# Attention sum with a fifth slot, experts' tiles gathered by a table of row numbers, message sum added straight into x

## The chip, the cores and the metric

One core of a Trainium2 chip runs the whole program. The metric is the device time of one execution in microseconds (us), the median of several. A core has five engines that run their own instruction streams: TensorE (PE, matrix products, results in PSUM), VectorE (DVE), ScalarE (ACT), GpSimd (POOL) and SyncE (SP), and 16 DMA engines that all queues share. Engines wait for one another by semaphores.

## The reference, cut to what matters

Two rounds of a graph network with a mixer and a feed-forward or expert layer, on 3125 nodes (rows) of 256 numbers with 50000 edges, sorted by their destination. Three parts matter here:

```
# first round: message sum
x = x + (normalised, weighted sum over the edges of rows of xn @ W) + mixer(xn)
# second round: attention over the edges
score = clip(einsum('ehd,ehd->eh', q[edge_dst], k[edge_src]) / sqrt(32), -10, 10)
ex = exp(score - smax[edge_dst]);  alpha = ex / segment_sum(ex)[edge_dst]
wv = segment_sum(alpha[:, :, None] * v[edge_src], edge_dst)
# last layer: a shared expert for all rows, and the best 2 of 8 experts per row
shared = gelu(x @ W1s + b1s) @ W2s + b2s
topw, topi = top_k(softmax(x @ Wr), 2);  topw = topw / sum(topw)
routed = sum over the two of topw * (gelu(x @ W1p[e] + b1p[e]) @ W2p[e] + b2p[e])
out = x + shared + routed
```

## The kernel before, in words

The 3125 rows lie in SBUF as T = 25 tiles of R = 125 partitions (`m.x`, `m.y`, `m.z`); J = 5 tiles are a chunk. The edges are G = 80 groups of J x R = 625. The program is a row of stages (`phase`), each a block in which every engine has its own loop; a barrier of all engines stands between stages.

**Start** (`graph_layers`, from L2857). SP loads x (L2861), then fills the DRAM table `pairs` with zeros by four transfers of 2 MB (L2865) from an area that DVE cleared (L2870). The stage ends when SP has issued all; POOL then writes the constants (L135 on), and `edge_tables` loads the edge lists (L182, L183), which DVE takes up at L189. The landings of x and of the fills are waited for after `edge_tables`.

**Message sum** (`message_sum`, L680). For each group POOL issues five indirect DMAs (L745), each of 125 gathered rows of 1 KB, into one of SLOTS = 4 slots. DVE writes the 0/1 matrix that says which edge goes to which of a tile's rows (`hot`, L769), PE multiplies it with the gathered rows (L812), and DVE adds the product to `summed` = `m.y` (`Adder.add`, L552), two visits behind PE. A group visits one or two tiles of destinations. Ahead of the loop stand a clearing of `m.y` (L752), one of PSUM (L753), and an iota of 3125 numbers on POOL (L738), ahead of the first index copies (L757). After the loop DVE adds `summed` times 1/sqrt(degree) to x in 25 instructions (L792). ACT and PE turn weights of later stages between the loop's five parts (`Turner`, loads L584, stores L613).

**Attention sum** (`attention_sum`, L1633). The same pattern with 2 KB rows of k and v in f32 (`gkv`, four slots; L1685). In turn n DVE multiplies q with k for group n+1 (L1818; q is picked by one-hots of ACT, L1732 and L1738, on PE, L1771 to L1784), reduces (L1823), clips (L1824), ACT takes the exponent (L1745), DVE copies the index for group n+3 (`next_index`, L1836) once PE is done with group n-1, writes the one-hot of group n (L1862), adds what PE summed (L552), and weighs v of group n+1 (L1830). PE sums group n (L1806). POOL gathers a group when its index is there. Ahead of it, q (3.2 MB, L1701) is loaded to SBUF from DRAM.

**Routing** (`routing`, L2337) scores the rows against the 8 experts and gives each of the 6250 (row, expert) pairs a place in a list in which each expert's pairs fill whole tiles of TN = 256, NT = 32 tiles in all (`m.place`, L2484).

**Experts** (`shared_and_experts`, L2488). POOL writes each row to its two places in the DRAM table `pairs` (L2534, 50 indirect DMAs). Meanwhile PE does SHARED_BEFORE = 3 chunks of the shared expert (`chunk`: up products L457 with gelu on ACT, L2696, and splitting into two f16 halves on DVE, L2749 and L2751; then down products, L2621, and DVE's addition to x, L2762). Then come the 32 tiles: SP loads rows (`load_rows`, L2562) and an expert's weights of 2 MB (L2552, four slots) ahead, PE turns the rows (`turn`, L2634; ACT copies them, L2703), and multiplies up and down; results go to DRAM (L2567). After the last tile PE does the other two chunks, POOL gathers the results of the two experts of every row back (L2544, GOT = 4 slots), and DVE joins them into x (`join`, L2771): seven tiles after the fourth chunk, the rest after the last. SP stores each tile of x when joined (L2599).

## Time and profile before

| | |
|---|---|
| median of 3 runs | 4137.75 us (4130.2 to 4140.1) |
| profiled execution | 4135.46 us, span 4133.7 us |
| busy: PE, DVE, ACT, POOL | 2615.2, 2172.5, 1260.5, 1312.0 us |
| start and edge tables | 0 to 130 |
| message sum | 253 to 914 |
| attention sum | 2388 to 3251 |
| routing | 3515 to 3558 |
| experts | 3558 to the end |

The profile is of one execution. Times in its rows are microseconds from the span's start unless a mean in ns is meant. The stage bounds above are read from the order of time. Where a row names a releaser (`<-`), that is what ended the idle time of the engine ahead of the instruction. Idle time of an engine that isn't what ends last costs nothing.

### The profile page before, as it was taken

Reading aid. Unit: us, or ns where it says so; the run is one execution under the profiler, and the core shown is the slowest. Engines: PE = TensorE matmul, PEld = TensorE weight load, DVE = VectorE, ACT = ScalarE, POOL = GpSimd, SP = SyncE. Lnnn points to the kernel's source line nnn. Section 1 sums busy time; section 2 is a strip of 40 time slices with the busy share of each in tenths; the row PEclk is TensorE's granted clock in tenths of the full one; section 3 lists DMA queues with packets and bytes.
Section 4 is the critical chain, followed back from the end, with each engine's and each line's share of the span. In section 5 each row is a group of like instructions: output and inputs, shape, how many; then the busy total and the mean of one; then the engine's idle time right before and its main releaser. Section 6 shows DMA issues by size and latency. Waiting matters only on the chain. (4 is left out here: it accounts for less than half of the span.)

```text
span 4133.7 us, 66642 instructions
## 1 busy us (share of the span) xinstructions
PE 2615.2 (63%) x17072; PEld 2109.2 (51%) x17073; DVE 2172.5 (53%) x4422; ACT 1260.5 (30%) x2441; POOL 1312.0 (32%) x996
## 2 busy tenths in 40 slices
PE   3513334437587799975654426666766487699993
PEld 2413333324276577753444325445545466589983
DVE  5623323231555488883347736666666655544443
ACT  0200000003244155551477512222222244244440
POOL 0038888842000000000001136667767500510015
PEclk9955555557688699987777658999888778799996
DMA  2036566730000000002000046666665100356643
GB/s 116 23 93 161 144 170 159 193 86 6 0 21 0 15 15 15 15 8 100 14 1 0 0 120 159 159 163 168 168 165 161 54 21 0 126 177 231 232 162 85
DMA packets 263746, 383.33 MB, mean 93 GB/s; under 512 B 122411, under 2 KB 189607, under 8 KB 258810
## 3 DMA queue, kind: packets, MB, share of 16 engines
q0 software_dynamic: 156960, 171.31, 16.8%
q1 hardware_dynamic: 93850, 199.08, 14.5%
q10 hardware_dynamic: 12864, 12.06, 1.0%
q8 instruction: 36, 0.59, 0.1%
q14 instruction: 36, 0.29, 0.0%
HBM read 318.81 MB, written 62.55 MB: 92 GB/s over the span
## 5 line engine op out<-in xcount | busy, mean ns | idle before, releaser
L1685 POOL DMA_INDIRECT as_gkv<-gather_kv,as_index x415 | 565.7, 1363 | 280.5 <-DVE as_index L1836 170.5
L745 POOL DMA_INDIRECT ms_got<-gather,ms_index x400 | 505.9, 1265 | 128.6 <-issue 109.3
L812 PE MATMUL ms_total<-ms_got,ms_hot 125*125 125x256 f16 x1040 | 231.7, 411 | 382.8 <-DMA ms_got<-gather,ms_index 292.9
L812 PEld LDWEIGHTS ms_total<-ms_got,ms_hot 125*125 x1040 | 203.6, 219 | 411.1 <-issue 411.1
L1806 PE MATMUL as_total<-as_gkv,as_hot 125*125 125x264 f32 x1040 | 280.0, 420 | 76.1 <-DVE as_summed L552 66.1
L2093 POOL MEMSET bm_fx<- 128x128 f32 x1 | 0.2, 204 | 1012.9 <-POOLq L114 1012.9
L1806 PEld LDWEIGHTS as_total<-as_gkv,as_hot 125*125 125x125 f32 x1040 | 201.2, 202 | 127.6 <-issue 91.4
L1479 ACT ACTIVATE ex_h<-ex_up,ex_now 128x313 f32<-128x313 f32 (+1 forms) x320 | 195.8, 612 | 197.6 <-PE ex_up L457 190.4
L2749 DVE CAST moe_hidden<-moe_h 128x256 f16<-128x256 f32 (+1 forms) x336 | 107.3, 319 | 206.2 <-ACT moe_h L2696 206.2
L1818 DVE TENSOR_TENSOR z_flat<-as_picked,as_gkv 125x1280 f32<-125x1280 f32 x81 | 120.4, 1487 | 176.7 <-DMA as_gkv<-gather_kv,as_index 130.2
L2696 ACT ACTIVATE moe_h<-moe_up,moe_w 128x256 f32<-128x256 f32 (+1 forms) x336 | 163.2, 486 | 140.3 <-PE moe_up L457 95.4
L1771 PE MATMUL as_picked<-y_rows,as_zeros 125*125 125x512 f16 (+1 forms) x246 | 72.5, 412 | 205.0 <-DVE z_flat L1818 147.3
L2544 POOL DMA_INDIRECT z_rows<-results,place x50 | 64.8, 1295 | 418.1 <-DMA results<-moe_made 374.3
L1780 PE MATMUL as_picked<-y_rows,as_pick 125*125 x1060 | 168.5, 316 | 44.5 <-issue 40.0
L1780 PEld LDWEIGHTS as_picked<-y_rows,as_pick 125*125 x1060 | 140.0, 155 | 80.2 <-issue 77.8
L2659 PE MATMUL moe_down<-moe_w,moe_hidden 128*128 128x256 f16 x1536 | 178.2, 273 | 0.0
L1745 ACT ACTIVATE as_gkv<-as_score 125x40 f32<-125x40 f32 x81 | 19.1, 236 | 510.8 <-DVE as_score L1824 510.8
L457 PE MATMUL moe_up<-moe_cols,moe_w 128*128 128x256 f16 x1536 | 172.9, 273 | 1.4 <-ACT moe_cols L2703 1.4
L1521 DVE TENSOR_TENSOR ex_h<-ex_h 128x313 f16<-128x313 f32 (+1 forms) x320 | 155.3, 485 | 11.0
L457 PEld LDWEIGHTS moe_up<-moe_cols,moe_w 128*128 128x128 f16 x1536 | 150.0, 98 | 19.1 <-issue 1.6
L670 ACT ACTIVATE ms_split<-ms_raw 128x1024 f16<-128x1024 f32 x36 | 37.6, 1054 | 399.7 <-DMA ms_raw<-in_L_ffn_W1p 358.8
L2659 PEld LDWEIGHTS moe_down<-moe_w,moe_hidden 128*128 128x128 f16 x1536 | 150.5, 98 | 17.2
(431 smaller groups left out, 5859.1 us busy)
## 6 DMA issues: line engine op xcount, KB each, us to landing
moe_w<-wsplit SPq DMA_DIRECT2D x34, 2052.0 KB
as_dsts<-in_dst SPq DMA_DIRECT2D x83, 305.2 KB
wsplit<-ms_split SPq DMA_DIRECT2D x36, 512.0 KB, 4.3
pairs<-z_flat SPq DMA_DIRECT2D x4, 2048.0 KB, 21.5
ms_raw<-in_L_ffn_W1p SPq DMA_DIRECT2D x16, 512.0 KB, 6.9
ms_raw<-in_L_ffn_W2p SPq DMA_DIRECT2D x16, 512.0 KB, 9.2
moe_rows<-pairs SPq DMA_DIRECT2D x32, 256.0 KB
results<-moe_made SPq DMA_DIRECT2D x32, 256.0 KB, 8.2
```

Of the source, the lines that this page charges most:

```text
L457: ins = pe.matmul(out, left(k, b), right(n, b), start=(i == 0), stop=(i == len(todo) - 1))
L745: pool.indirect_dma_start(out=got[:, s, j, :], out_offset=None, in_=m.gather0, in_offset=bass.IndirectOffsetOnAxis(ap=index[:, s, j:j + 1] ...
L812: ins = pe.matmul(total[:, visit % RING, 0:C], hot[:, visit % RING, j, :], got[:, s, j, p * C:(p + 1) * C], start=(j + p == 0), stop=(j + ...
L1479: act.activation(h32[:, u % 4, 0:n], up[:, u % 4, 0:n], ACT.Relu, bias=now[:, 1, layer, o:o + 1], scale=now[:, 0, layer, o:o + 1]).then_in ...
L1521: dve.tensor_tensor(to[:, 1, o, at:at + n], full, to[:, 0, o, at:at + n], ALU.subtract).then_inc(s_h, 1)
L1685: pool.indirect_dma_start(out=gkv[:, s, j, 0:2 * C], out_offset=None, in_=m.gather_kv, in_offset=bass.IndirectOffsetOnAxis(ap=index[:, s, ...
L1780: ins = pe.matmul(picked[:, j // 2, at:at + C], pick[:, visit % PICKS, j * R:(j + 1) * R], q16[:, tile, p, :], start=False, stop=False)
L1806: ins = pe.matmul(total[:, visit % RING, 0:W], hot[:, s, j, :], gkv[:, s, j, C:C + W], start=(j == 0), stop=(j == J - 1))
L1818: dve.tensor_tensor(qk[:, :].rearrange("p (j c) -> p j c", j=J), picked[:, :, :].rearrange("p b c -> p (b c)")[:, 0:J * C] .rearrange("p ( ...
L2659: ins = pe.matmul(down[:, h, 0:C], hidden[:, k, f, h * 128:(h + 1) * 128], part(s, r, 1, f, 0, C), start=False, stop=(f == FB - 1 and n == 2))
L2696: act.activation(h32[:, u % 4, 0:n], up[:, u % 4, 0:n], ACT.Gelu, scale=1.0 / WS, bias=bias(s, f)).then_inc(s_h32, 1)
L2749: dve.tensor_copy(hidden[:, 0, f, at:at + n], full).then_inc(s_hhigh, 1)
```

## The change

1. The fills of `pairs`, the table itself and the clearing behind them go. `x` is the only load of the first stage.
2. Message sum: `Adder` takes a scale and adds straight into `m.x`; `m.y` isn't cleared, the pass L792 goes, and the one-hot is made from `m.row_no` plus a tile's first number, so that the long iota becomes one of 25.
3. Attention sum: five slots. Four lie in `gkv`, the fifth in an unused part of `z_cols`. ACT's loop has ten turns in its body, since its other buffers alternate by two.
4. Routing stores the rows (`m.rows16`) to the DRAM table `gather0` and splits each place into a block of 128 and a place in it (`m.spot`).
5. Experts: after the first shared chunk DVE and ACT make one-hots from `m.spot`, PE multiplies them (50 matmuls) into a table that holds the row number for each of the 8192 places, and POOL gathers each tile's rows by it, two indirect DMAs per tile, four slots. SHARED_BEFORE is 2, so that three chunks come after the experts. GOT is 12, and the joins stand between the units of the last three chunks.

```diff
-SHARED_BEFORE = 3
+SHARED_BEFORE = 2
+BLOCKS = NT * HN
...
-        dve.tensor_tensor(into, into, fresh, ALU.add).then_inc(self.s_added, 1)
+        if self.scale is None:
+            dve.tensor_tensor(into, into, fresh, ALU.add).then_inc(self.s_added, 1)
+        else:
+            dve.scalar_tensor_tensor(out=into, in0=fresh, scalar=self.scale[:, bass.ds(oldest, 1)], in1=into,
+                                     op0=ALU.mult, op1=ALU.add).then_inc(self.s_added, 1)
...
-        node_no = ph.sb("node_no", [R, N])
+        node = ph.sb("node", [R, T])
...
-                pool.iota(node_no[:, :], pattern=[[1, N]], base=0, channel_multiplier=0,
+                pool.iota(node[:, :], pattern=[[R, T]], base=0, channel_multiplier=0,
...
-                dve.memset(summed[:, :, :], 0.0).then_inc(s_zero, 1)
...
-                            dve.tensor_tensor(hot[:, visit % RING, :, :],
-                                              repeat_mid(node_no[:, bass.ds(tile * R, R)], J),
-                                              repeat_last(m.edge_dst[:, g, :], R), ALU.is_equal)\
-                                .then_inc(s_hot, 1)
+                            dve.scalar_tensor_tensor(out=hot[:, visit % RING, :, :],
+                                                     in0=repeat_mid(m.row_no[0:R, :], J),
+                                                     scalar=node[:, bass.ds(tile, 1)],
+                                                     in1=repeat_last(m.edge_dst[:, g, :], R),
+                                                     op0=ALU.add, op1=ALU.is_equal).then_inc(s_hot, 1)
...
-                with dve.Fori(0, CHUNKS) as c:
-                    for j in range(J):
-                        t = c * J + j
-                        dve.scalar_tensor_tensor(out=m.x[:, t, :], in0=summed[:, t, :],
-                                                 scalar=m.inv_sqrt_degree[:, bass.ds(t, 1)], in1=m.x[:, t, :],
-                                                 op0=ALU.mult, op1=ALU.add).then_inc(s_zero, 1)
...
+        SLOTS = 5
+        index = ph.sb("index", [R, SLOTS, J], I32)
         W = C + X8
-        index = ph.sb("index", [R, SLOTS, J], I32)
-        gkv = ph.sb("gkv", [R, SLOTS, J, C + W])
+        most = ph.sb("gkv", [R, SLOTS - 1, J, C + W])
+
+        at = J * R // 2 + 1
+        gkv = [most[:, s, :, :] for s in range(SLOTS - 1)]
+        gkv.append(m.z_cols[0:R, 1, at:at + J * (C + W)].rearrange("p (j w) -> p j w", j=J))
...
-                with act.Fori(0, G // SLOTS) as i:
-                    for s in range(SLOTS):
-                        n = i * SLOTS + s
+                with act.Fori(0, G // (2 * SLOTS)) as i:
+                    for s in range(2 * SLOTS):
+                        n = i * (2 * SLOTS) + s
                         bounds = group_bounds(act, m, n + 3)
                         weights(n + 1, (s + 1) % SLOTS)
-                        one_hots(n + 3, i * 2 + (s + 3) // 2, (s + 3) % 2, bounds)
+                        one_hots(n + 3, i * SLOTS + (s + 3) // 2, (s + 3) % 2, bounds)
 
             @block.tensor
...
+                sp.dma_start(m.gather0.rearrange("(t p) n -> p t n", p=R),
+                             m.rows16.rearrange("p t k c -> p t (k c)")).then_inc(s_rows, 16)
...
+                v.link(dve.tensor_scalar(m.spot[:, 0, :, :], stat[:, :, :], 1.0 / 128, 0.5 / 128 - 0.5,
+                                         ALU.mult, ALU.add))
+                v.link(dve.tensor_scalar(m.spot[:, 0, :, :], m.spot[:, 0, :, :], RNE, RNE, ALU.add, ALU.subtract))
+                v.link(dve.scalar_tensor_tensor(out=m.spot[:, 1, :, :], in0=m.spot[:, 0, :, :], scalar=-128.0,
+                                                in1=stat[:, :, :], op0=ALU.mult, op1=ALU.add))
...
-        GOT = 4
+        GOT = 12
...
-                for t in range(T):
-                    for k in range(2):
+                pool.iota(number[:, :], pattern=[[1, 128]], base=0, channel_multiplier=0,
+                          allow_small_or_imprecise_dtypes=True).then_inc(s_number, 1)
+                pool.iota(own[:, :], pattern=[[0, 1]], base=0, channel_multiplier=1,
+                          allow_small_or_imprecise_dtypes=True).then_inc(s_number, 1)
+                pool.wait_ge(s_taken, 1)
+                for i in range(NT):
+                    s = i % RINGW
+                    if i >= RINGW:
+                        pool.wait_ge(s_turned, i - RINGW + 1 + AHEAD)
+                    for h in range(HN):
+                        at = i * HN + h
                         pool.indirect_dma_start(
-                            out=m.pairs, out_offset=bass.IndirectOffsetOnAxis(ap=m.place[:, k, t:t + 1], axis=0),
-                            in_=rows16[:, t, :, :].rearrange("p k c -> p (k c)"), in_offset=None).then_inc(s_spread, 16)
-                pool.wait_ge(s_spread, 32 * T)
...
-                def load_rows(i, s):
-                    sp.dma_start(rows[:, s, :, :], m.pairs.rearrange("(i h p) n -> p i h n", h=HN, p=128)
-                                 [:, bass.ds(i, 1), :, :].rearrange("p i h n -> p (i h) n")).then_inc(s_rows[s], 16)
...
+                    if c == 0:
+                        pe.wait_ge(s_marked, T + 1)
+                        pe.wait_ge(s_block, 1 + J)
+                        pe.wait_ge(s_added, J + AHEAD)
+                        for n in range(2 * T):
+                            k, t = n // T, n % T
+                            ins = pe.matmul(down[:, 2, 0:2 * BLOCKS], in_block[:, k, t, :],
+                                            marked[:, k, t, :, :].rearrange("p a n -> p (a n)"),
+                                            start=(n == 0), stop=(n == 2 * T - 1))
+                        ins.then_inc(s_inverse, 1)
+                        pe.wait_ge(s_taken, 1)
...
+                    if c == 0:
+                        act.wait_ge(s_number, 2)
+                        act.wait_ge(s_block, 1)
+                        act.activation(marked[:, :, :, 0, :].rearrange("p k t n -> p (k t) n"),
+                                       of_block[:, :, :, :].rearrange("p k t n -> p (k t) n"), ACT.Copy,
+                                       scale=own[:, 0:1]).then_inc(s_marked, 1)
+                        for t in range(T):
+                            act.activation(marked[:, :, t, 1, :], of_block[:, :, t, :], ACT.Copy,
+                                           scale=float(t)).then_inc(s_marked, 1)
...
+                def blocks(j):
+
+                    some = slice(j * 2 * T // J, (j + 1) * 2 * T // J)
+                    if j == 0:
+                        dve.wait_ge(s_number, 2)
+                        dve.tensor_tensor(of_block[:, :, :, :].rearrange("p k t n -> p (k t) n"),
+                                          repeat_mid(number[0:R, 0:BLOCKS], 2 * T), repeat_last(spots[0], BLOCKS),
+                                          ALU.is_equal).then_inc(s_block, 1)
+                    dve.tensor_tensor(in_block[:, :, :, :].rearrange("p k t n -> p (k t) n")[:, some, :],
+                                      repeat_mid(number[0:R, :], 2 * T // J), repeat_last(spots[1][:, some], 128),
+                                      ALU.is_equal).then_inc(s_block, 1)
...
-                    add(c)
+                    add(c, blocks if c == 0 else None)
+                    if c == 0:
+                        dve.wait_ge(s_inverse, 1)
+                        dve.tensor_copy(row_of[:, :], down[:, 2, 0:BLOCKS]).then_inc(s_set, 1)
+                        dve.wait_ge(s_set, 2)
+                        dve.scalar_tensor_tensor(out=row_of[:, :], in0=down[:, 2, BLOCKS:2 * BLOCKS], scalar=float(R),
+                                                 in1=row_of[:, :], op0=ALU.mult, op1=ALU.add).then_inc(s_set, 1)
+                        dve.wait_ge(s_set, 3)
+                        dve.tensor_copy(taken[:, :], row_of[:, :]).then_inc(s_taken, 1)
...
+                joins = iter(range(T))
+
+                def join_next(u):
+
+                    if u % 2 == 1:
+                        t = next(joins)
+                        join(t, 0)
+                        join(t, 1)
+
                 for c in range(SHARED_BEFORE, CHUNKS):
                     dve.wait_ge(s_down, c * J + AHEAD)
-                    halves_of(UB + NT * FB + (c - SHARED_BEFORE) * units, units, of_chunk)
+                    dve.wait_ge(s_added, c * J + AHEAD)
+                    halves_of(UB + NT * FB + (c - SHARED_BEFORE) * units, units, of_chunk,
+                              join_next if c > SHARED_BEFORE else lambda u: u >= units // 2 and join_next(u))
                     add(c)
-                    upto = T if c == CHUNKS - 1 else T * (c + 1 - SHARED_BEFORE) // (AFTER + 1)
-                    if c == CHUNKS - 1:
-                        dve.wait_ge(s_added, CHUNKS * J + AHEAD)
-                    for t in range(done, upto):
-                        join(t, 0)
-                        if t > done:
-                            join(t - 1, 1)
-                    join(upto - 1, 1)
-                    done = upto
+                dve.wait_ge(s_added, CHUNKS * J + AHEAD)
+                for t in joins:
+                    join(t, 0)
...
-        FILLS = 4
-        with nc.semaphore("x_in") as s_x, nc.semaphore("clear") as s_clear, nc.semaphore("filled") as s_filled:
+        with nc.semaphore("x_in") as s_x:
             with nc.Block() as block:
 
                 @block.sync
                 def _(sp):
                     sp.dma_start(m.x[:, :, :], a["x"].rearrange("(t p) n -> p t n", p=R)).then_inc(s_x, 16)
-                    sp.wait_ge(s_clear, 1)
-                    for i in range(FILLS):
-                        n = NT * TN // FILLS
-                        sp.dma_start(m.pairs[i * n:(i + 1) * n, :].rearrange("(p k) n -> p (k n)", p=128),
-                                     z_flat[:, 0:n * 2 * C // 256].bitcast(F16)).then_inc(s_filled, 16)
-
-                @block.vector
-                def _(dve):
-                    dve.memset(z_flat[:, 0:NT * TN // FILLS * C // 128], 0.0).then_inc(s_clear, 1)
```

## Rows read from the trace of the kernel before

**Rows 1.** Order of time, 0 to 60: start, duration, engine, line, operation [idle before].

```profile
0.81 0.36 SPq L2861 DMA_DIRECT2D x_rows<-in_x  x1
...
5.23 23.12 SPq L2865 DMA_DIRECT2D pairs<-z_flat  x4
28.76 0.20 POOL L135 MEMSET ident<- 128x128 f32 x1 [27.50 <-POOLq L2857]
...
50.92 0.81 DVE L189 CAST edg_rawf<-edg_raw 80x1250 f32<-80x1250 int32 x1 [45.71 <-DMA edg_raw<-in_src]
```

**Rows 2.** Busy by engine in stretches: us, PE, PEld, DVE, ACT, POOL, clock, DMA share, GB/s.

```profile
10.00:20.00 10.00, 0.00 (x0) 0.00 (x0) 0.00 (x0) 0.00 (x0) 0.00 (x0) 1.00 0.34 118
...
2450.00:3236.00 786.00, 519.45 (x2560) 397.06 (x2560) 505.12 (x610) 189.75 (x289) 547.45 (x400) 0.89 0.61 162
...
4040.00:4080.00 40.00, 26.56 (x195) 20.97 (x193) 21.16 (x52) 8.35 (x16) 20.64 (x16) 0.79 0.29 78
```

**Rows 3.** Order of time, 250 to 264, ahead of the message sum's loop.

```profile
253.99 5.39 DVE L752 MEMSET y_rows<- 125x6400 f32 x1 [17.55 <-issue]
...
262.88 1.38 POOL L745 DMA_INDIRECT ms_got<-gather,ms_index  x1 [7.08 <-DVE ms_index L757]
```

**Rows 4.** Groups by line, 264 to 900: count | busy us, mean ns | idle before.

```profile
L745 POOL DMA_INDIRECT ms_got<-gather,ms_index x400 | 505.9, 1265 | 128.6 <-issue 109.3 <-DVE ms_index L779 12.2 <-DVE ms_index L757 7.1
...
L769 DVE TENSOR_TENSOR ms_hot<-ms_node_no,edge_dst x104 | 84.5, 812 | 103.0 <-issue 103.0
```

**Rows 5.** Order of time, 890 to 915, end of the message sum.

```profile
894.26 2.36 PE L812 MATMUL ms_total<-ms_got,ms_hot 125*125 125x256 f16 x10 [5.40 <-DMA ms_got<-gather,ms_index]
...
897.89 9.98 DVE L792 SCALAR_TENSOR_TENSOR x_rows<-y_rows,inv_sqrt_degree,x_rows  x25 [0.47 <-DVE y_rows L552]
...
909.57 0.37 ACTq L613 DMA_DIRECT2D turned_res<-ms_cols  x1
```

**Rows 6.** Groups by line, 2450 to 3236, the loop of the attention sum.

```profile
L1685 POOL DMA_INDIRECT as_gkv<-gather_kv,as_index x400 | 547.5, 1369 | 275.7 <-DVE as_index L1836 170.5 <-issue 105.3
...
L1818 DVE TENSOR_TENSOR z_flat<-as_picked,as_gkv 125x1280 f32<-125x1280 f32 x80 | 118.9, 1487 | 130.7 <-DMA as_gkv<-gather_kv,as_index 130.2 <-PE as_picked L1784 0.4
...
L1862 DVE SCALAR_TENSOR_TENSOR as_hot<-row_no,as_node,edge_dst 125x625 f32<-125x625 f32 x104 | 90.7, 872 | 124.5 <-PE as_total L1806 80.4 <-issue 44.0
```

**Rows 7.** Order of time, 2806 to 2809, inside that loop.

```profile
2806.10 1.48 DVE L1830 TENSOR_TENSOR as_gkv<-as_gkv 125x1280 f32<-125x1280 f32 x1
...
2806.31 2.35 POOL L1685 DMA_INDIRECT as_gkv<-gather_kv,as_index  x1 [0.30 <-issue]
```

**Rows 8.** Order of time, 2388 to 2455 and 3240, the loop's edges.

```profile
2388.72 0.29 SPq L1701 DMA_DIRECT2D y_rows<-gather_q  x1
...
2436.43 1.32 PE L1771 MATMUL as_picked<-y_rows,as_zeros 125*125 125x512 f16 x3 [57.56 <-DMA y_rows<-gather_q]
...
2454.12 1.65 POOL L1685 DMA_INDIRECT as_gkv<-gather_kv,as_index  x1 [41.67 <-DVE as_index L1836]
...
3240.04 0.36 DVE L1874 TENSOR_SCALAR as_gkv<-as_summed 125x200 f32<-125x200 f32 x1 [7.66 <-DMA as_gkv<-gather_kv,as_index]
```

**Rows 9.** Chain that ended last, 3550 to 4134: start, us, what.

```profile
3636.79 11.02 PE moe_down L2621 x99
```

**Rows 10.** Groups by line, 3480 to 4134.

```profile
L2703 ACT ACTIVATE moe_cols<-moe_turned 128x1024 f16<-128x1024 f16 x32 | 32.7, 1023 | 15.2 <-PE moe_turned L2634 13.4
...
L2771 DVE SCALAR_TENSOR_TENSOR x_rows<-z_rows,share,x_rows 125x256 f32<-125x256 f32 x50 | 21.5, 482 | 42.4 <-DMA z_rows<-results,place 42.4
```

**Rows 11.** Order of time, 4013 to 4017, after the last expert tile.

```profile
4013.56 12.97 PE L457 MATMUL moe_up<-z_flat,moe_w 128*128 128x313 f16 x96 [0.52 <-issue]
...
4016.56 1.38 POOL L2544 DMA_INDIRECT z_rows<-results,place  x1 [374.28 <-DMA results<-moe_made]
```

**Rows 12.** Order of time, 4082 to 4134, the end.

```profile
4082.69 0.42 DVE L2762 SCALAR_TENSOR_TENSOR x_rows<-moe_down,x_rows 125x256 f32<-125x256 f32 x1 [2.20 <-PE moe_down L2621]
...
4127.94 1.28 DVE L2771 SCALAR_TENSOR_TENSOR x_rows<-z_rows,share,x_rows 125x256 f32<-125x256 f32 x3 [1.38 <-DMA z_rows<-results,place]
```

74 lines of the change are left out of this document (42 added, 32 removed).

## The prediction

> **What bounds the kernel now.** I read the page first (slices and chain), then one stage at a time: the list of costly lines and waits inside each stage the change touches, and the order of time at the stage's edges. The program is a row of stages with a barrier between them, so what counts is what ends last in each.
>
> Start: the load of x is issued at 0.81, four fills of `pairs` hold SP's queue from 5.23 to 28.35, POOL starts its constants only at 28.76, and VectorE (DVE) gets the edge lists at 50.92 after 45.71 us of waiting for that load [rows 1]. While x is alone, the DMA engines are busy 0.34 of the time and move 118 GB/s [rows 2].
>
> Message sum: POOL's 400 gathers take 505.9 us, with 109.3 us between them and 19.3 us of waits on DVE [rows 4], in a loop of 634 us. POOL is the bound; work of DVE there is hidden. At the stage's end the DVE pass over x (897.89 to 907.87) ends before the weight turner's last store is even issued, at 909.57, and the turner hangs on TensorE's (PE's) last group at 894.26 [rows 5].
>
> Attention sum: 786 us for 80 groups (2450 to 3236 [rows 2]), 9.8 per group. POOL is busy 547.5, between gathers 105.3, and waits 170.5 for an index [rows 6], 41.7 of it at the start [rows 8]; DVE waits 130.2 for gathered rows [rows 6]. Each waits for the other: a ring too short, no engine full. An index for group n+3 is written in the middle of turn n, and its rows are wanted at the start of turn n+2. With a period P that leaves 2P less some 3.5 us; the gather takes 5 x 1.63 on POOL, about 1 to start and 4.3 to land after the last (below), some 14 to 15.5 with queueing: P of 9 to 9.5, near the 9.8 seen.
>
> Experts: PE is full from the first chunk to the experts' end at 4013.04; then two chunks of shared work with joins, the last addition at 4083.11, and 18 tiles still to join; the last join ends at 4129.2, the span at 4133.7 [rows 9, 11, 12]. The tail is POOL's gathers and the wait of DVE for them.
>
> **Part by part.**
>
> *Fills of `pairs` gone.* The first stage's barrier now waits for nothing long, so the edge lists are asked for near 4 to 5 us instead of 31. What is late next is x's load: 3.2 MB at 118 GB/s [rows 2] is 27.1 us, from about 3 us on; the edge lists lie behind it in the same queue and land at about 32. Gain 50.9 - 32 = 19. Ends: 14 if the load begins slowly, 38 if the lists get past x (then only barriers and a short load remain, some 13 us). I take 19. The share of 0.34 is 5.4 of 16 engines [rows 2]; the Trainium skill, "DMA: Bandwidth & Descriptors", section "Why a DMA increments its semaphore by 16 and not by 1", says that a transfer is spread over the largest k up to 16 that divides both slowest dims, so 125 partitions get 5, and 80 get 16. By that rule the lists' packets on those 5 engines queue behind x; the row agrees with 5 engines.
>
> *Message sum, front.* The memset of y (5.39) goes from in front of the index copies [rows 3]; the 3125-wide iota, which ran beside it, goes too. All gathers start 5.4 earlier, and POOL-bound work keeps that. In the loop the one-hot becomes a scalar_tensor_tensor (872 ns each in the attention sum [rows 6] against 812 now [rows 4]), 104 x 0.06 = 6 us on an engine with slack: 0. The addition with a scale costs some 0.06 more, hidden by the same POOL work; with the cover gone it would be 6 + 6 us. The DVE pass of 9.98 at the end is worth 0, because the turner ends later [rows 5]. Sum -5.4, ends -8 and +10 (the second if the new one-hot lengthens POOL's gathers by 0.15 each time).
>
> *Attention sum, fifth slot.* Now 3P less 3.5 must cover the same 15.5: 6.3, no bound any more. DVE alone would need 786 - 130 = 656 us, 8.2 per group. POOL: a gather that nothing disturbs is 1.21 (the shortest; the mean in the message sum is 1.265 [rows 4]) plus 0.30 between [rows 7], 1.51; it is longer when a DVE instruction with two SBUF inputs runs as it starts: 2.35 at 2806.31, begun 0.21 after L1830 [rows 7]. The mean is 1.369 [rows 6], the excess over 1.21 400 x 0.159 = 63.6 us, met while POOL was active for (547.5 + 105.3) / 786 = 0.83 of the loop; active all the time it meets 63.6 / 0.83 = 76. So POOL needs 400 x 1.51 + 76 = 680, more than DVE's 656: POOL becomes the bound, at 8.5 per group. It starts that loop at 2454.12 [rows 8], later by what a fourth group of gathers costs the load of q: that load would take 27 us alone (3.2 MB at 118 GB/s [rows 2]) and took 47.7 beside 15 gathers (2388.72 to 2436.43 [rows 8]), 1.4 us for each, so 5 more cost 6.9. POOL ends at 2454.1 + 6.9 + 680 = 3141.0. The rows land 4.3 later: from the first gather of the loop at 2454.12 to the end of the last wait at 3240.04 [rows 8] are 785.9 us, of which 547.5 + 105.3 is POOL's work and 128.8 its waits in the loop (170.5 - 41.7). So 3145.3 against 3240.0, -94.7. I give back 3 for turns with two visits, in which DVE is late: -92 (rounded). The fourth unused group at the end is in the 400. Ends: -125 (DVE the bound at 656, with its tail) and -55 (P stays at 9.1).
>
> The Trainium skill's "SBUF — State Buffer", section "Who interferes with whom", says that a DVE instruction with two SBUF inputs contends with a GpSimd instruction that reads SBUF. The trace agrees (2.35 against 1.21). By it the gain is 12 us smaller than with POOL's present mean.
>
> *Routing.* Three DVE operations on 50 columns, each waited for, at the end: one on 200 columns takes 0.36 (L1874 [rows 8]), so at most 1.1 for three, and +0.7 taken for 50 columns each, ends 0.3 and 1.5. The store of 3.2 MB of rows takes some 28 us at the pace of rows 2, and the stage is 43 us long by the table ahead: 0; uncovered, up to 5.
>
> *Experts, one shared chunk moved behind.* A chunk is 12.97 up [rows 11] and 120 x 11.02/99 = 13.3 down [rows 9]: -26.3 ahead of the experts.
>
> *Experts, table of row numbers.* From the end H of the first chunk's DVE halves: `of_block` has 3200 columns at 1.16 ns (1485 for 1280 [rows 7]; 872 for 625): 3.6. Then ACT: one of 3200 at 0.8 to 1.0 ns, 2.8, and 25 of 128 at 0.31 (between a fixed 0.2 and 1023 for 1024 [rows 10]): 7.8. Ready at H + 14.2, while PE's down phase ends at H + 11.1 [rows 9]. 50 matmuls at 0.11 at most [rows 9]: 5.5. Three small DVE operations with waits 1.2. PE goes on at H + 20.9, +9.8; ends 6 and 16 (slower small ACT instructions, lower clock). The gathers of rows, 2 for each tile, run four tiles ahead on an idle POOL with 11.4 us per tile ((4013.0 - 3647.8) / 32 [rows 9, 11]): 0.
>
> *Tail, from T = 4013.04.* DVE's unit is 0.85 beside gathers, a tile's two joins 0.96 [rows 10]. POOL starts at T+3.5 [rows 11] and gives a tile each 3.4 us. Third-to-last chunk: the first join waits for T+11.2, the fourth ends T+22.4, halves end 23.3, PE's down 34.5. The next two: 1.5 + 16 x 0.85 + 8 x 0.96 + 11.0 = 33.8 each, to T+102.1. Then 0.5, five tiles 4.8, the last store 4.5 (as now): T+112 against T+120.7, -9. Ends -16 and +20. The twelve slots let POOL finish near T+90, so it no longer ends last.
>
> **Sum.** -19 - 5.4 - 92 + 0.7 - 26.3 + 9.8 - 9 = -141.2. The profiled run took 4135.46 for a span of 4133.7; 4135.5 - 141.2 = 3994.3, and the median shown, 4137.75, is 2.3 above that run: **3996**.
>
> **Rivals.**
> *Port costs nothing more (P down to DVE's 8.2).* For it: the two engines may fall in step, as they do now where DVE works while POOL waits. -125 in the attention sum instead of -92: 3963. Against: 185 DVE instructions with two SBUF inputs have nowhere to hide.
> *Edge lists pass x.* -38 instead of -19: 3977.
> *PE's clock falls in the tail.* Joins leave PE idle in each up phase, 8 to 10 us. Down phases at half speed: 3 x 11 = 33, and up phases that end 4 later: +45, 4041. For it: between 4040 and 4080, where PE stands still for some 13 us, the granted clock is 0.79 on the mean, so part of it at the lower of the two levels, 1.2 instead of 2.4 GHz [rows 2]. Against: the new stalls come in pieces under 2 us.
> *Fifth slot brings nothing* (landings lengthen with the load, or a hidden wait of PE or ACT takes over): 3996 + 92 = 4088. For: PE is 519 us busy of 786, DVE 505. Against: neither is near the whole, and the DMA share is 0.61 [rows 2].
> *Slower than before: the experts' weights come late.* Rows in 1 KB pieces on POOL's queue share the 16 DMA engines with 2 MB of weights for every tile. It decides when a tile's weights need more than 11.4 us; at 15.9 per tile, 32 x 4.5 = 144 us, the whole gain is gone: 4140, and any more is slower. Against: now the same rows and weights are read, and PE takes 365 us for the 32 tiles, from 3647.81 [rows 9] to 4013.04 [rows 11], with hardly a gap.
>
> **How the numbers follow.** Forecast 0.60 (3970 to 4022), port rival 0.09, edge lists 0.08, clock in the tail 0.14, nothing from the slot 0.06, weights 0.03 (half of it slower). The range 3962 to 4036 leaves out the last two, and part of the clock's. What a measurement here can tell from no change is 0.3%, 12 us: faster 0.97, same 0.01, slower 0.02.
>
> **What would show it.** DVE's first edge operation at 32; message sum's first gather 24 us earlier, near 238.5, its last DVE pass gone and the end still the turner's; POOL in the attention sum waiting under 10 us for indices in the loop, a mean above 1.40 us, DVE's wait for rows down to some 40, loop near 690; a hole of 8 to 11 us on PE after the first chunk; PE's end 4 to 8 us before the span's. It is wrong if POOL still waits for indices, or if the tail after the experts takes over 121.

## The result, and the profile after

The changed kernel takes **3985.89 us** (median of 4 runs, 3984.23 to 3990.22), the kernel before 4138.93 in the same comparison (4130.20 to 4141.86): ratio 0.9635, 95% interval 0.9618 to 0.9652. The forecast was 3996 with a range of 3962 to 4036. The profiled execution took 3987.43 for a span of 3985.7, 148.0 less than before.

How much earlier the changed kernel is at the edges of the stages:

| edge | before | after | earlier by | of it in this stretch |
|---|---|---|---|---|
| DVE's first edge operation [rows 1] | 50.92 | 31.94 | 19.0 | -19.0 |
| message sum, first gather [rows 3] | 262.88 | 237.58 | 25.3 | -6.3 |
| message sum, turner's last store [rows 5] | 909.57 | 885.45 | 24.1 | +1.2 |
| attention sum, first gather | 2389.98 | 2370.07 | 19.9 | +4.2 |
| attention sum, end of the last wait [rows 8] | 3240.04 | 3121.01 | 119.0 | -99.1 |
| routing, start | 3514.92 | 3395.17 | 119.7 | -0.7 |
| experts, first turned tile | 3647.65 | 3507.11 | 140.5 | -20.8 |
| experts, end (T) | 4013.04 | 3872.50 | 140.5 | 0.0 |
| span's end | 4133.7 | 3985.7 | 148.0 | -7.5 |

Order of time, changed kernel, 0 to 34 and 234 to 239 (start, duration, engine, line, operation [idle before]); these answer to [rows 1, 3]:

```profile
0.81 0.35 SPq L2931 DMA_DIRECT2D x_rows<-in_x  x1
...
1.62 0.20 POOL L136 MEMSET ident<- 128x128 f32 x1 [0.36 <-POOLq L2927]
...
4.23 20.72 SPq L183 DMA_DIRECT2D edg_raw<-in_dst  x1
25.00 0.42 SPq L184 DMA_DIRECT2D edg_raw<-in_src  x1
31.94 0.81 DVE L190 CAST edg_rawf<-edg_raw 80x1250 f32<-80x1250 int32 x1 [31.82 <-DMA edg_raw<-in_src]
...
234.50 1.76 DVE L757 MEMSET ms_total<- 125x2048 f32 x1 [16.52 <-PEq L115]
...
236.30 0.31 DVE L761 COPY ms_index<-edge_src 125x5 int32<-125x5 int32 x3
237.58 1.38 POOL L750 DMA_INDIRECT ms_got<-gather,ms_index  x1 [2.94 <-DVE ms_index L761]
```

The first stage no longer waits for the fills (POOL's constants stand at 1.62 instead of 28.76), and DVE gets the lists at 31.94, as forecast. One thing wasn't in the forecast: behind x's load the issue of the first list alone holds SP's queue for 20.72 us, so the second list is only asked for at 25.00.

The attention sum, groups by line, 2430 to 3125 (count | busy us, mean ns | idle before and what ended it). The fifth slot lies in `z_cols`, which the view names `z_flat`, so its gathers and products have lines of their own; together they answer to [rows 6]:

```profile
L1689 POOL DMA_INDIRECT as_gkv<-gather_kv,as_index x320 | 437.7, 1368 | 102.3 <-issue 94.6 <-DVE as_index L1840 7.8
L1689 POOL DMA_INDIRECT z_flat<-gather_kv,as_index x80 | 110.2, 1377 | 63.9 <-DVE as_index L1840 39.7 <-issue 24.2
...
L1822 DVE TENSOR_TENSOR z_flat<-as_picked,as_gkv 125x1280 f32<-125x1280 f32 x65 | 96.6, 1485 | 72.6 <-PE as_picked L1788 52.0 <-DMA as_gkv<-gather_kv,as_index 20.1 <-issue 0.5
...
L1866 DVE SCALAR_TENSOR_TENSOR as_hot<-row_no,as_node,edge_dst 125x625 f32<-125x625 f32 x104 | 90.6, 871 | 120.5 <-issue 61.7 <-PE as_total L1810 58.8
...
L1822 DVE TENSOR_TENSOR z_flat<-as_picked,z_flat 125x1280 f32<-125x1280 f32 x16 | 23.8, 1485 | 3.4 <-DMA z_flat<-gather_kv,as_index 3.4
```

POOL's waits for an index fell from 128.8 us in the loop to 7.8 (the 39.7 are the start), DVE's for rows from 130.2 to 23.5 (20.1 + 3.4). POOL is at work nearly all the time: 437.7 + 110.2 busy and 94.6 + 24.2 between gathers. The edges, order of time [rows 8]:

```profile
2368.82 0.29 SPq L1705 DMA_DIRECT2D y_rows<-gather_q  x1
...
2422.08 1.32 PE L1775 MATMUL as_picked<-y_rows,as_zeros 125*125 125x512 f16 x3 [63.12 <-DMA y_rows<-gather_q]
...
2439.86 1.65 POOL L1689 DMA_INDIRECT z_flat<-gather_kv,as_index  x1 [39.68 <-DVE as_index L1840]
...
3113.10 1.21 POOL L1689 DMA_INDIRECT as_gkv<-gather_kv,as_index  x1 [0.31 <-issue]
3121.01 0.36 DVE L1878 TENSOR_SCALAR as_gkv<-as_summed 125x200 f32<-125x200 f32 x1 [13.27 <-DMA as_gkv<-gather_kv,as_index]
```

From PE's first matmul to the start of POOL's last gather, "the loop" below, it is 798.0 us before and 691.0 after. In the traces of the fills back, the lists first, q in two transfers, both of these together and the chunk in front (all below), whose loops have the same instructions, it is 683.5 to 696.3: a difference of under some 13 us between two loops shows nothing by itself.

The table of row numbers and the tail, order of time, changed kernel [rows 9, 11, 12]:

```profile
3469.64 5.08 ACT L2758 ACTIVATE z_rows<-rowvec 125x128 f16<-125x128 f16 x25
...
3475.55 2.95 PE L2694 MATMUL moe_down<-z_rows 125*128 125x128 f16 x50 [0.61 <-DVE x_rows L2820]
...
3479.31 2.97 PE L458 MATMUL moe_up<-z_flat,moe_w 128*128 128x313 f16 x21 [0.81 <-DVE moe_taken L2845]
...
3869.83 2.67 PE L2680 MATMUL moe_down<-moe_w,moe_hidden 128*128 128x256 f16 x23
...
3875.99 1.45 POOL L2577 DMA_INDIRECT z_rows<-results,place  x1 [63.00 <-DMA results<-moe_made]
...
3907.02 0.42 DVE L2820 SCALAR_TENSOR_TENSOR x_rows<-moe_down,x_rows 125x256 f32<-125x256 f32 x1 [2.20 <-PE moe_down L2642]
...
3941.68 0.42 DVE L2820 SCALAR_TENSOR_TENSOR x_rows<-moe_down,x_rows 125x256 f32<-125x256 f32 x1 [2.20 <-PE moe_down L2642]
...
3975.54 0.42 DVE L2820 SCALAR_TENSOR_TENSOR x_rows<-moe_down,x_rows 125x256 f32<-125x256 f32 x1 [2.19 <-PE moe_down L2642]
3976.00 4.67 DVE L2829 SCALAR_TENSOR_TENSOR x_rows<-z_rows,share,x_rows 125x256 f32<-125x256 f32 x10
```

PE stands for 0.61 + 0.81 and works 2.95 for the table, a hole of 4.4. T, the end of the experts' last matmul, is 3872.50 here. The last additions of the three chunks end at T+34.9, T+69.6 and T+103.5, then five tiles are joined without a wait.

### The profile page after: what moved, and what is told of

It is laid out like the page before. It is cut to its first block and busy times, and to the rows that moved or that the text cites. A ratio compares the mean times of both kernels' runs of the same rounds, so it can differ in the third digit from the quotient of the medians.

```text
span 3985.7 us, 66521 instructions
## 1 busy us (share of the span) xinstructions
PE 2587.3 (65%) x17122; PEld 2086.2 (52%) x17123; DVE 2170.5 (54%) x4408; ACT 1269.1 (32%) x2467; POOL 1315.5 (33%) x1017
## 3 DMA queue, kind: packets, MB, share of 16 engines
q1 hardware_dynamic: 87700, 185.50, 14.2%
## 5 line engine op out<-in xcount | busy, mean ns | idle before, releaser
L750 POOL DMA_INDIRECT ms_got<-gather,ms_index x400 | 506.2, 1265 | 124.9 <-issue 114.4
L1689 POOL DMA_INDIRECT as_gkv<-gather_kv,as_index x340 | 462.0, 1359 | 108.7 <-issue 100.9
L1810 PE MATMUL as_total<-as_gkv,as_hot 125*125 125x264 f32 x850 | 218.8, 406 | 78.0 <-DVE as_summed L555 65.6
L1810 PEld LDWEIGHTS as_total<-as_gkv,as_hot 125*125 125x125 f32 x850 | 157.7, 193 | 117.8 <-issue 91.8
L1784 PE MATMUL as_picked<-y_rows,as_pick 125*125 x1060 | 150.3, 291 | 52.6 <-issue 47.7
L1784 PEld LDWEIGHTS as_picked<-y_rows,as_pick 125*125 x1060 | 123.9, 141 | 87.3 <-issue 84.5
L2567 POOL DMA_INDIRECT moe_rows<-gather,moe_taken x64 | 63.0, 984 | 309.9 <-PE moe_turned L2655 259.8
L1866 DVE SCALAR_TENSOR_TENSOR as_hot<-row_no,as_node,edge_dst 125x625 f32<-125x625 f32 x104 | 90.6, 871 | 120.5 <-issue 61.7
L2793 DVE TENSOR_TENSOR moe_hidden<-moe_h,moe_hidden 128x256 f16<-128x256 f32 (+1 forms) x336 | 148.3, 441 | 11.6
L458 PE MATMUL ex_down<-ex_w,ex_h 128*125 128x256 f16 x1200 | 148.1, 276 | 2.3
```

The costliest lines, as they stand in the source:

```text
L458: ins = pe.matmul(out, left(k, b), right(n, b), start=(i == 0), stop=(i == len(todo) - 1))
L750: pool.indirect_dma_start(out=got[:, s, j, :], out_offset=None, in_=m.gather0, in_offset=bass.IndirectOffsetOnAxis(ap=index[:, s, j:j + 1] ...
L1689: pool.indirect_dma_start(out=gkv[s][:, j, 0:2 * C], out_offset=None, in_=m.gather_kv, in_offset=bass.IndirectOffsetOnAxis(ap=index[:, s, ...
L1784: ins = pe.matmul(picked[:, j // 2, at:at + C], pick[:, visit % PICKS, j * R:(j + 1) * R], q16[:, tile, p, :], start=False, stop=False)
L1810: ins = pe.matmul(total[:, visit % RING, 0:W], hot[:, s, j, :], gkv[s][:, j, C:C + W], start=(j == 0), stop=(j == J - 1))
L2793: dve.tensor_tensor(hidden[:, 1, f, at:at + n], full, hidden[:, 0, f, at:at + n], ALU.subtract).then_inc(s_hidden, 1)
```

## The experiments

Every ratio is to the kernel before, run on the same chip in the same comparison; the changed kernel's is 0.9635. Trace numbers are of one profiled execution each.

**One part back: four slots**

```
-        SLOTS = 5
+        SLOTS = 4
```

> The changed kernel with four slots in the attention sum in place of five (the fourth then lies in z_cols). Theory: the ring's length was the bound. POOL waits for indices again, near 130 us in the loop, DVE for rows near 130 us; the loop takes 785 us in place of 687, the whole 4085 us (4078 to 4092). Rival: the stage got faster through the place of the slots or through its start; then the loop stays under 720 and the whole under 4015.

Measured: 4107.02, ratio 0.9908 (0.9882 to 0.9934), the loop 806.1.

```profile
L1689 POOL DMA_INDIRECT as_gkv<-gather_kv,as_index x253 | 350.2, 1384 | 163.2 <-DVE as_index L1840 95.7 <-issue 67.5
...
L1822 DVE TENSOR_TENSOR z_flat<-as_picked,as_gkv 125x1280 f32<-125x1280 f32 x52 | 77.4, 1488 | 69.2 <-DMA as_gkv<-gather_kv,as_index 67.6 <-issue 0.7 <-PE as_picked L1788 0.4
```

(Groups by line, 2430 to 3110; the gathers and products of the fourth slot are lines of their own.) Both old waits are back: over the whole loop POOL waits 129.3 us for indices, near the 130 expected. The slot alone carries 0.027 of the ratio, some 113 of the 153 us, and the rival that it brings nothing falls, as does the one that the place of the slots or the start did it. The loop is 21 us and the total 22 us longer than expected, outside the range given; why, no run shows.

**Is DVE the next bound?** The reduction over 1280 numbers is left out, 40 of its inputs are copied instead.

```
-   v.link(dve.tensor_reduce(score[:, :], qk[...], AX_X, ALU.add))
+   v.link(dve.tensor_copy(score[:, :], qk[:, 0:J * X8]))
```

> The changed kernel, with the reduction of q*k in the attention sum left out (the scores are 40 columns of the product, copied; 1.3 us less of DVE in each of 80 turns). Theory: POOL is the bound now, so the loop stays at 677 to 692 us, DVE's waits for rows grow by about 100 us, the whole is 3976 to 3992. Rival: DVE is the bound; then the loop falls by about 100 us to 585, the whole to 3885.

Measured: 3993.61, ratio 0.9635 (0.9609 to 0.9662); the loop 697.4. DVE has 102 us less to do (some 80 times 1486 to 224 ns), and nothing is gained; loop and total end just above the expected 692 and 3992. The number fits POOL as the bound, and DVE's work isn't it. But POOL waits 28.5 us for indices in the loop here, and DVE has new waits (below), so the run alone doesn't prove it.

**The port's price taken away.** The weights of `weigh` are ones in PSUM, so that this instruction has one SBUF input.

```
-   dve.tensor_tensor(rows, rows, repeat_last(gkv[s][:, :, 2 * C:C + W], HD), ALU.mult)
+   dve.tensor_tensor(rows, rows, repeat_mid(spare[:, 0:C], J), ALU.mult)
```

> The changed kernel, where the weighing of v multiplies by ones in PSUM instead of by the exponents in SBUF (same size, one SBUF input instead of two; v is not weighed). Theory: DVE instructions with two SBUF inputs lengthen the gathers that start beside them. POOL's mean falls from 1.37 to 1.22 to 1.27 us, POOL needs about 620 us, DVE and PE bound the loop at 645 to 665, the whole is 3950 to 3967. Rival: the gathers are long because the DMA queue is full; then the mean stays near 1.37, the loop near 687, the whole near 3986.

Measured: 4020.25, ratio 0.9699 (0.9671 to 0.9727): a miss. The first half, the shorter gathers, holds. These are the groups of the loop, 2430 to 3110:

```profile
L1690 POOL DMA_INDIRECT as_gkv<-gather_kv,as_index x301 | 377.5, 1254 | 151.3 <-issue 88.6 <-DVE as_index L1840 62.7
...
L1867 DVE SCALAR_TENSOR_TENSOR as_hot<-row_no,as_node,edge_dst 125x625 f32<-125x625 f32 x100 | 88.0, 880 | 137.0 <-remote 60.1 <-PE as_total L1811 41.1 <-issue 35.8
```

The mean gather fell from 1368 to 1254 ns, about 46 us over 400. It came back as POOL's waits for an index (83.6 us in the loop instead of 7.8), and the loop took 718.4, 27.4 more. The Trainium skill, "SBUF — State Buffer", section "Who interferes with whom", says that a DVE instruction with two SBUF inputs contends with a GpSimd instruction that reads SBUF, as a gather reads its index there; the mean here agrees, but what the stage gains isn't in that rule.

**The fills back.** Four transfers of 2 MB and their clearing, as in the kernel before, to a table that nothing reads.

```
+   for i in range(FILLS):
+       sp.dma_start(m.pairs[i * n:(i + 1) * n, :]..., z_flat[...].bitcast(F16)).then_inc(s_filled, 16)
```

> The changed kernel with the four fills of 2 MB back in the first stage (and the clearing ahead of them; nothing reads them). Theory: the fills alone held the edge lists; DVE's first edge operation is at 50.9 again, the whole is 19 us longer, 4005 (4001 to 4009). Rival: the load of x bounds the start in both; then the whole stays at 3986 to 3990.

Measured: 4004.48, ratio 0.9658 (0.9634 to 0.9682). DVE's first edge operation is at 50.95 and the first gather of the message sum at 256.58, both 19.0 later than in the changed kernel. The span is 8.7 longer only, since the same loop of the attention sum took 683.5 in this execution instead of 691.0. So the 19 us are shown by the trace; the ratios (0.0023 apart, intervals that overlap) don't tell 9 from 19.

**q in two transfers**

```
-   sp.dma_start(q16..., m.gather_q...).then_inc(s_q, 16)
+   for lo, hi in ((0, 120), (120, R)):
+       sp.dma_start(q16...[lo:hi], m.gather_q...[lo:hi]).then_inc(s_q, 16)
```

> The changed kernel with the load of q in the attention sum cut in two transfers, partitions 0 to 119 and 120 to 124 (3.2 MB in all, as before). Theory (a transfer of 125 partitions runs on few of the 16 DMA engines, 0.34 of their time and 118 GB/s in the rows of before, while 80 or 120 partitions spread over more): q lands 10 to 30 us after the stage's first gather instead of 53, the loop's first gather comes 25 to 40 us sooner, the ratio to the kernel before falls from 0.9635 to 0.954 to 0.958. Rival (q is late because the gathers of four groups take the DMA engines' time, whichever way q is cut): q still lands after 48 to 55 us and the ratio stays at 0.9635.

Measured: 3976.46, ratio 0.9596 (0.9564 to 0.9628): between the two. Busy in the stretch 2380 to 2390 (us, PE, PEld, DVE, ACT, POOL, clock, DMA share, GB/s), first the changed kernel, then this one:

```profile
2380.00:2390.00 10.00, 0.00 (x0) 0.00 (x0) 0.00 (x0) 0.00 (x0) 7.86 (x8) 0.50 0.83 208
```

```profile
2380.00:2390.00 10.00, 0.00 (x0) 0.00 (x0) 0.00 (x0) 0.00 (x0) 7.86 (x8) 0.50 1.12 195
```

The share adds up the times of packets, which overlap, so it can pass 1. In these 10 us SP's queue, that of the load, moved 0.81 MB instead of 0.39, and POOL's gathers 1.14 instead of 1.70: the load got more, but out of the gathers' part, and the sum didn't rise. q is there 35 us after the first gather instead of 52. Then PE waits for something else, 8.86 us:

```profile
2405.03 1.32 PE L1776 MATMUL as_picked<-y_rows,as_zeros 125*125 125x512 f16 x3 [46.17 <-DMA y_rows<-gather_q]
...
2412.79 0.82 ACT L1737 ACTIVATE z_flat<-as_dsts,as_minus_node 125x625 bf16<-125x625 int32 x1 [47.80 <-DMA as_dsts<-in_dst]
...
2415.21 2.36 PE L1785 MATMUL as_picked<-y_rows,as_pick 125*125 x10 [8.86 <-ACT as_pick L1743]
```

The destination numbers, asked for behind q, land last; the loop's first gather comes 12 us sooner, not 25 to 40.

**Edge lists ahead of x**

```
+   sp.dma_start(raw[:, 0, :], a["dst"]...).then_inc(s_lists, 16)
+   sp.dma_start(raw[:, 1, :], a["src"]...).then_inc(s_lists, 16)
    sp.dma_start(m.x[:, :, :], a["x"]...).then_inc(s_x, 16)
```

> The changed kernel with the two edge lists (0.8 MB) asked for ahead of x in the first block. Theory (the lists were late only because they stood behind x in the same queue): DVE's first edge operation at 7 to 12 us instead of 31.9, everything after it 20 to 25 us sooner, ratio 0.9575 to 0.959. Rival (x is what the next stage needs as well, so it only moves the wait to the layernorm): first edge operation early, but the message sum's first gather still at 237 and the ratio at 0.9635.

Measured: 3964.06, ratio 0.9578 (0.9543 to 0.9613), as expected. Order of time of this kernel, 0 to 6:

```profile
0.81 0.40 SPq L2926 DMA_DIRECT2D raw_lists<-in_dst  x1
1.26 0.41 SPq L2927 DMA_DIRECT2D raw_lists<-in_src  x1
1.73 0.35 SPq L2928 DMA_DIRECT2D x_rows<-in_x  x1
...
5.17 0.81 DVE L184 CAST edg_rawf<-raw_lists 80x1250 f32<-80x1250 int32 x1 [5.06 <-PEq L115]
```

The first gather of the message sum is at 211.26, 26.3 sooner: nothing of it is lost. The lists land before the barriers are through.

**The shared chunk back in front**

```
-SHARED_BEFORE = 2
+SHARED_BEFORE = 3
```

> The changed kernel with three shared chunks ahead of the experts and two behind, as the kernel before had it; the rest of the change stays. Theory: ahead of the experts +26.3; behind them the tail loses one chunk of 33.8 us, but POOL, which gathers a tile's two rows in 3.4 us, then sets the end at T+3.5+85 and 13 tiles are left to join, so T+97 instead of T+113, -16; total +10, ratio 0.9660. Rival (the tail follows PE alone, the joins are not the limit): T+80, total -7, ratio 0.962. Rival 2 (my +26.3 is wrong since something else, say the experts' weights, set the experts' start): ratio 0.9595.

Measured: 3994.51, ratio 0.9642 (0.9611 to 0.9674). The experts end at 3899.2, 26.7 later (expected +26.3), the span at T+94.9 (expected T+97). DVE's last joins wait for POOL again:

```profile
3987.36 1.00 DVE L2829 SCALAR_TENSOR_TENSOR x_rows<-z_rows,share,x_rows 125x256 f32<-125x256 f32 x2 [2.23 <-DMA z_rows<-results,place]
3988.70 1.01 DVE L2829 SCALAR_TENSOR_TENSOR x_rows<-z_rows,share,x_rows 125x256 f32<-125x256 f32 x2 [0.33 <-DMA z_rows<-results,place]
```

So taking the move back costs 26.7 - 18.3 = 8.4 us in the span, less than the comparison of the ratios can show: most of the gain ahead of the experts is paid again behind them.

**Both edits together**

> Both edits together, edge lists ahead of x and the load of q cut in 120 + 5 partitions. If both theories hold the gains add: 45 to 65 us under the changed kernel, ratio 0.948 to 0.9525. If only the lists' holds: 0.958.

Measured: 3948.14, ratio 0.9537 (0.9505 to 0.9569), just above the expected 0.948 to 0.9525. The span is 39.4 us shorter than the changed kernel's; the lists' run alone gave 25.1 and q's 8.9, together 34 of the 39.4.

**A busier PE**, once with ones in PSUM, once in the changed kernel. Eight matmuls of zeros in each turn, into a bank that is overwritten:

```
    pick_q(n + 2, ahead)
+   next_visit = pe.snap(before)
+   pe.wait_ge(s_added, next_visit + 1)
+   for _ in range(8):
+       pe.matmul(total[:, next_visit % RING, 0:C], zeros[:, :], q16[:, 0, 0, :], start=True, stop=True)
```

> The kernel with weigh's second input in PSUM again (ones instead of the weights), plus eight matmuls of 256 columns with zero weights in each turn of the attention sum, between the picked rows and the sum of the turn, into a bank of `total` that is free by then and is overwritten afterwards; only TensorE gets more work. Theory (the gathers' shorter mean did not pay there because TensorE, standing still more often, ran 19 of 99 visits at the lower clock and DVE waits for each): slow visits fall to under 8, the loop ends 25 to 45 us sooner than without the eight, ratio 0.959 to 0.964 against 0.9699. Rival (the waits of 5 to 6.7 us come from elsewhere, say the POOL's index arriving late, and the slow matmuls only follow from them): slow visits fewer, but the loop as long or longer, ratio 0.9695 or more.

> The changed kernel with the same eight matmuls a turn and nothing else. Theory (POOL is the bound and only 6 of 100 visits are slow, 9 us in all): between 9 us faster and 3 us slower, ratio 0.961 to 0.9645. Rival (TensorE's own time is on the path in each turn): 80 x 0.9 = 70 us slower, ratio 0.980.

Measured: 3974.01, ratio 0.9600 (0.9569 to 0.9631), and 3982.45, ratio 0.9629 (0.9600 to 0.9658). With ones in PSUM the loop falls from 718.4 to 681.4. Busy in 2450 to 3050, ones in PSUM without and with the eight:

```profile
2450.00:3050.00 600.00, 427.24 (x2200) 327.21 (x2201) 438.91 (x521) 161.75 (x246) 429.90 (x343) 0.93 0.74 182
```

```profile
2450.00:3050.00 600.00, 485.72 (x2906) 384.70 (x2905) 458.72 (x548) 171.70 (x261) 453.08 (x362) 0.98 0.79 192
```

In the changed kernel the granted clock is 0.97 over the same stretch, 0.99 with the eight, and PE's busy time rises there from 428.6 to 482.0 us at no cost to the total. So both expectations hold in their numbers. Whether the reason given in the first one holds is taken up at the last run below.

**All four edits.** The real weights go to PSUM by a second Exp; with lists, q and the eight matmuls.

```
+   act.activation(weight[:, 0:J * X8], score[:, :], ACT.Exp).then_inc(s_exp, 1)
    act.activation(gkv[s][:, :, 2 * C:C + W], ..., ACT.Exp).then_inc(s_exp, 1)
...
-   dve.wait_ge(s_exp, g + 1)
+   dve.wait_ge(s_exp, 2 * g + 2)
```

> The changed kernel with edge lists ahead of x, the load of q cut in 120 + 5 partitions, the weights of the attention sum written by ACT to PSUM as well (a second Exp of 40 columns) and read from there by weigh, and the eight matmuls a turn that keep TensorE busy. The first two gave 0.9537 together. Theory: the last two take what they took from the changed kernel with ones in PSUM, 0.9635 to 0.9600, so the ratio is 0.948 to 0.952 and POOL's mean gather 1.25 to 1.26 us. Rival (the second Exp and its wait delay weigh, DVE becomes late in every turn): ratio 0.9537 or more.

Measured: **3926.89** (3924.46 to 3932.55), ratio **0.9494** (0.9478 to 0.9509), as expected and the best of the study, 0.014 or 58 us under the changed kernel. The mean gather of the loop is 1.25 us. Against both edits together the loop is 682.2 instead of 694.1: of the 46 us that the gathers lost, at most 12 show in the loop, while POOL's waits for an index rose from 7.0 to 56.1.

**Destination numbers ahead of q**, in that version:

```
+   for s in range(2): load(s, s)
    for lo, hi in ((0, 120), (120, R)): sp.dma_start(q16...)
-   for s in range(2): load(s, s)
```

> The version with all four edits, and in the attention sum the first two loads of destination numbers (305 KB each, for ACT's one-hots) asked for ahead of q. Theory (with q cut in two the next thing that comes late is this load: q is there 33.6 us after the stage's first gather and PE then stands for the one-hot until 41 us or more): the loop's first index comes 6 to 11 us sooner, ratio 0.9465 to 0.948 against 0.9494. Rival (the DMA engines are full until then, so what goes first only pushes q back by as much): within 3 us, 0.949 to 0.950.

Measured: 3995.87 (3975.48 to 4028.12), ratio 0.9647 (0.9599 to 0.9695): outside both expectations. q now lands 51 us after the first gather, and in its trace the loop takes 734.0 instead of 682.2, although its instructions are the same. The two versions ran on different chips, and on this one the kernel before spread over 34 us as well, instead of 15. Order of time in it, in a turn with two visits:

```profile
2660.37 0.42 DVE L549 TENSOR_TENSOR as_summed<-as_summed,as_total  x1
...
2660.78 2.48 PE L1811 MATMUL as_total<-as_gkv,as_hot 125*125 125x264 f32 x10 [0.31 <-DVE as_hot L1867]
...
2665.77 0.87 DVE L1867 SCALAR_TENSOR_TENSOR as_hot<-row_no,as_node,edge_dst 125x625 f32<-125x625 f32 x1 [4.98 <-remote]
```

The one-hot of the second visit needs PE's product of the first. By the row PE ends at 2663.26; in the changed kernel DVE starts 0.3 us after such an end, here 2.5 (the view names no instruction as releaser). Over the 24 such turns and all 104 visits of each trace:

| kernel | loop, us | DVE's mean idle ahead of the second one-hot, us | turns in which it starts over 0.6 us after PE's end | visits over 2.8 us | all visits, us |
|---|---|---|---|---|---|
| changed kernel | 691.0 | 3.10 | 0 | 6 | 267.7 |
| short reduction | 697.4 | 4.59 | 13 | 19 | 286.4 |
| ones in PSUM | 718.4 | 4.54 | 16 | 21 | 295.0 |
| the same, busier PE | 681.4 | 3.02 | 0 | 1 | 255.4 |
| busier PE alone | 686.7 | 2.98 | 0 | 1 | 254.5 |
| all four edits | 682.2 | 3.00 | 0 | 2 | 255.0 |
| destination numbers first | 734.0 | 4.17 | 10 | 19 | 288.2 |

The three kernels that disappointed share this late start, 24 x 1.45 = 35 us for two of them and 24 x 1.2 = 28 us against its own base for the third. For that one the visits also took 33 us longer in all; with the 28 that is more than the 52 us by which its loop is longer.

I had taken the clock for the cause in the expectation of the busier PE. The order of events speaks against it. In the turn shown PE had the eight matmuls and the granted clock was 1.00 in 2660 to 2666; it fell only after the stall, to a mean of 0.69 in 2666 to 2671 (1.2 GHz for part of it). In 35 of the 39 late turns of the three kernels the product before the late start took 2.49 us or less, and in 35 of them the product after it took 3.4 us or more. So the slower clock follows the late start and adds to its price, and the busier PE with ones in PSUM may owe its gain to either. Ends of matmuls are modelled (their starts stand an even 0.22 us apart up to 2662.88), so the trace doesn't tell whether PE ended late or DVE began late.

What causes the late start stays open. The chip alone isn't it: four slots and the fills back ran on the same chip as the short reduction and the ones in PSUM and have one such turn each. That the eight matmuls remove it, or that the order of two loads brings it, isn't shown either, since each of these pairs is one trace against one from another chip.

## Why the prediction was right, and where its terms were off

*Fills, -19.* Measured -19.0, and again +19.0 with the fills back. The mechanism was x's load in front of the lists, and the run that turns the order round confirms it: asked for first, the lists are there at 5.17. The rival, that the lists pass x, didn't come. What the forecast didn't have is that x's load also holds back the issue of the lists, for 20.72 us.

*Message sum, -5.4 and 0 for the pass.* Measured -6.3 ahead of the loop and +1.2 in it: the costlier DVE instructions stay hidden, gathers have a mean of 1265 ns as before.

*Attention sum, -92.* Measured -99.1: the right step, a little small. It splits in +5.6 for q (47.7 to 53.3; forecast +6.9), -107.0 in the loop and +2.3 at the landing. POOL needed 547.9 + 118.8 = 666.7, not 680: the port's lengthening stayed at 0.160 us a gather (64 us for 400) instead of growing to 76. So the step from "met 0.83 of the time" to "met all the time" was wrong, and with it the sign of a mean above 1.40 us; it is 1.370. The rival in which the port costs nothing more, with -125, didn't come either. POOL's waits of 7.8 us, against the 3 given back for turns with two visits, eat part of those 13. That POOL is the bound now is shown by its waits of 7.8 us, and DVE's work isn't by the short reduction. That the next bound lies close below is shown by POOL's waits once its gathers are shorter: 83.6 us with ones in PSUM, 56.1 with all four edits.

*Experts, one chunk less in front, -26.3 + 9.8 + 0.7 = -15.8.* Measured -20.8. The chunk itself was right: put back in front it costs 26.7. The table's hole was mis-sized: 4.4 instead of 9.8. The 25 small ACT instructions are 0.29 us long but overlap, so that one starts every 0.20, where I took 0.31; the 50 matmuls took 2.95 instead of 5.5. What was ready at H + 14.2 in the forecast was ready when the down phase ended. From the start of routing to PE's first product of the experts it is 0.5 us less than before, where +0.7 was forecast; against that, the phases of the two chunks that stay are some 2 us longer.

*Tail, -9.* Measured -7.5. The additions end at T+34.9, 69.6, 103.5 (forecast 34.5, 68.3, 102.1), the rest takes 9.7 (forecast 9.8). The sign "PE's end 4 to 8 us before the span's" didn't come: it is 10.2, as the forecast's own sum has it. The rival of a falling clock didn't come: 0.91 in 3940 to 3980 against 0.79 in the corresponding stretch [rows 2].

*The unchanged stages.* +4.2 between the message sum's end and the attention sum had no term. Between their first gathers lie 2127.1 us before and 2128.4 to 2135.8 in the thirteen traces of the changed kernel and its variants; the cause isn't settled.

*Experts' weights late.* 365.4 us from the first turned tile to T, as before.

The total is right by its large terms, the slot and the chunk. That it fits so closely is partly luck: 5 us more than forecast came ahead of the experts and 7 in the attention sum, while 4 were lost in stages that I took as unchanged, 1.2 in the message sum's loop and 1.5 in the tail. With smaller ones, 6.8 us more gain in the span than forecast are left, 148.0 instead of 141.2. The other 4 us between 3996 and 3986 lie in the step from the profiled run to the median: +2.3 before, -1.5 after.

## What to carry to other kernels

When two engines wait for each other around a ring, count the slots in periods, and then add up the next bound before promising more: here the fifth slot gave 0.027 of the time, and the next 46 us taken off POOL shortened the loop by 12 at best and came back as waits otherwise. An early load that is late costs in full, so look at the order in which SP issues before looking at loops: two lines moved gave 25 us. And a term that moves work from before a stage to behind it (27 us) has to be read with what it costs behind (18 us).
